# Normalisation, routing and row transfers of a sorted expert stage, moved into the attention before it

## The reference, cut to what matters

```python
x = x + _L1_xattn_ref(_layernorm(x), ctx, ctx, mask, ...)  # 16 heads of 64, keys 64 per batch
x = x + _L1_ffn_ref(_layernorm(x), ...)

def _L1_ffn_ref(x, gate_w, w1, w3, w2):     # 8 experts of width 512, two per token
    probs = softmax(x @ gate_w)
    expert_weights, expert_indices = top_k(probs, 2)
    expert_weights = expert_weights / expert_weights.sum(-1, keepdims=True)
    for i in range(8):
        wi = where(expert_indices == i, expert_weights, 0).sum(-1)
        out = out + (silu(x @ w1[i]) * (x @ w3[i])) @ w2[i] * wi[..., None]
```

## Time and profile before

| | us |
|---|---|
| median of 3 runs (lowest, highest) | 1563.43 (1560.48, 1563.63) |
| the profiled execution: its time | 1563.46 |
| its span, first to last instruction | 1561.6 |
| TensorE busy | 1265.0 (81%) |
| VectorE busy | 986.5 (63%) |
| ScalarE busy | 723.0 (46%) |
| GpSimd busy | 625.1 (40%) |

### The profile page before, as it was taken

One profiled execution on the slowest core, in us unless ns is written; L12 is line 12 of the kernel. 1 busy time (PEld: TensorE's weight loads), 2 busy tenths in 40 slices (PEclk: granted clock), 3 DMA queues, 4 the chain that ended last, 5 costly groups with the idle time before them and its releaser, 6 DMA issues. The chain is left out here.

```text
span 1561.6 us, 24205 instructions
## 1 busy us (share of the span) xinstructions
PE 1265.0 (81%) x7182; PEld 1030.1 (66%) x7182; DVE 986.5 (63%) x2041; ACT 723.0 (46%) x1276; POOL 625.1 (40%) x614
## 2 busy tenths in 40 slices
PE   5976499997996899712997596999945759999997
PEld 3873388887564699711886285788723548787875
DVE  6546688885324467560665655677668777777775
ACT  3444367664332555331554253555433325555553
POOL 3205443340000233154333332299824127676665
PEclk9997699997997999855999698799956569999999
DMA  7800011100000000221111620222212024343433
GB/s 202 205 1 0 21 36 41 40 25 0 0 1 0 21 1 0 81 100 52 40 45 32 174 42 21 69 81 87 83 42 84 1 73 129 114 129 116 126 116 102
DMA packets 77282, 98.89 MB, mean 63 GB/s; under 512 B 15226, under 2 KB 41213, under 8 KB 77194
## 3 DMA queue, kind: packets, MB, share of 16 engines
q1 hardware_dynamic: 73490, 92.69, 20.5%
q0 software_dynamic: 2272, 4.24, 0.8%
q10 hardware_dynamic: 1440, 0.98, 0.3%
HBM read 77.87 MB, written 14.16 MB: 59 GB/s over the span
## 5 line engine op out<-in xcount | busy, mean ns | idle before, releaser
L2675 POOL TENSOR_TENSOR e_h<-e_h,e_gate 128x512 f32<-128x512 f32 x128 | 187.9, 1484 | 143.8 <-DVE e_h L2727 87.9
L2732 DVE TENSOR_TENSOR e_h_low<-e_h,e_h_high 128x512 fp32r<-128x512 f32 x132 | 117.2, 888 | 74.4 <-ACT e_h_high L2662 74.2
L2662 ACT ACTIVATE e_h_high<-e_h 128x512 fp32r<-128x512 f32 x132 | 83.5, 633 | 95.8 <-POOL e_h L2675 88.1
L2727 DVE TENSOR_TENSOR e_h<-e_s,e_ps_b 128x512 f32<-128x512 f32 x132 | 89.3, 677 | 13.1 <-ACT e_s L2647 7.2
L1320 PE MATMUL u_ps_o<-u_vaug,u_pT 128*128 128x72 f32 x768 | 97.1, 270 | 0.0
L1320 PEld LDWEIGHTS u_ps_o<-u_vaug,u_pT 128*128 128x128 f32 x768 | 93.5, 192 | 0.0
L2647 ACT ACTIVATE e_s<-e_ps_a 128x512 f32<-128x512 f32 x132 | 77.7, 589 | 31.0 <-PE e_ps_a L1683 27.4
L1251 POOL TENSOR_TENSOR u_kbd<-u_keys,groupmask 96x512 fp32r<-96x512 f32 x60 | 62.9, 1067 | 62.4 <-DMA u_keys<-s_k 36.9
L1347 ACT ACTIVATE u_sm<-u_sm 128x512 f32<-128x512 f32 x96 | 60.6, 631 | 53.5 <-DVE u_sm L1379 52.8
L1377 DVE TENSOR_REDUCE u_mx<-u_ps_s 128x2 f32<-128x512 f32 (+1 forms) x96 | 66.2, 689 | 21.1 <-PE u_ps_s L1302 20.3
L2123 POOL DMA_INDIRECT sorted_y<-e_y,e_zb x39 | 37.8, 970 | 89.8 <-DVE e_y L2328 87.4
(11 more groups left out here) (474 smaller groups left out, 3894.4 us busy)
## 6 DMA issues: line engine op xcount, KB each, us to landing
e_gate<-gates_by_expert SPq DMA_DIRECT2D x256, 128.0 KB, 2.9
e_gate<-gates_by_expert SPq DMA_DIRECT2D x32, 256.0 KB, 3.2
a_q<-q_part SPq DMA_DIRECT2D x24, 256.0 KB, 6.4
w_raw<-in_L1w SPq DMA_DIRECT2D x24, 256.0 KB, 4.9
u_qs<-s_q SPq DMA_DIRECT2D x16, 192.0 KB, 2.6
u_keys<-s_k SPq DMA_DIRECT2D x8, 384.0 KB, 3.5
w_w<-in_L2w SPq DMA_DIRECT2D x24, 128.0 KB, 2.6
sorted<-blank SPq DMA_DIRECT2D x1, 2535.0 KB, 15.7
```

What stands on the lines that cost most here:

```text
L2662: nc.scalar.activation(h_parts[k % 3][0][:, :], h[k % 3][:, :], ACT.Copy).then_inc(high_ready, 1)
L2675: nc.gpsimd.tensor_tensor(h[c % 3][:, :], h[c % 3][:, :], gate[pair % SLOTS][:, :], ALU.mult)\
L2727: nc.vector.tensor_tensor(h[c % 3][:, :], s[c % 3][:, :], ps_b[c % 3][:, :], ALU.mult)\
L2732: nc.vector.tensor_tensor(h_parts[k % 3][1][:, :], h[k % 3][:, :], h_parts[k % 3][0][:, :], ALU.subtract).then_inc(low_ready, 1)
```

## The change

Layer norm, routing and transfers are taken apart into groups of four tiles and put into the steps of `attend_wide` by a new class `Router`, which each engine's program calls at (on TensorE: within) its step. Each expert has a fixed region of 2048 rows in `sorted`, so the place of a row needs only the counts of earlier groups; `table` gets a second row with each block's place in DRAM, which SP reads into a register for each block's load. The root becomes Ln and Exp on ScalarE with three operations on VectorE. To free a PSUM bank for the router, the transposes of the probabilities go through one bank in two halves. The blanks grow to 17280 rows. The wide attention's weights are loaded in the normalisation before it and no longer at the start of the program; the raw expert weights are loaded during the attention. Group 3 and the transfers from tile 8 on come after the attention. In the blocks, silu writes into `h`, there are four row buffers, TensorE spins on eight matmuls before the first rows, and a block waits only for the weights of the experts up to its own number.

```diff
+REGION = B * S
+SORTED_ROWS = SORT_E * REGION + (SORT_E - 1) * P
...
+class Router:
+    STEPS = 8
+    AFTER = 4
...
+    def dve(self, dve, t):
+        nc = self.nc
+        if 4 <= t < TILES + 4:
+            dve.drain()
+            nc.vector.bn_stats(self.stats[:, t - 4, :], self.x[:, t - 4, :])
+        if t % 4 == 3 and 7 <= t < TILES + 4:
+            self.variance(dve, (t - 7) // 4)
+        if t % 4 == 0 and 8 <= t < TILES + 8:
+            self.normal_rows(dve, (t - 8) // 4)
+        if t % 4 == 2 and 10 <= t < TILES + 8:
+            self.pick(dve, (t - 10) // 4)
+        if t % 4 == 3 and 11 <= t < TILES + 8:
+            self.places(dve, (t - 11) // 4)
+        if t == TILES + 7:
+            self.block_table(dve)
...
+    def normal_rows(self, dve, g):
+
+        nc, h = self.nc, self.tiles(g)
+        dve.wait_ge(self.root_ready, g + 1)
+        nc.vector.tensor_tensor(self.half[:, h], self.root[:, h], self.root[:, h], ALU.mult)
...
+        for t in range(h.start, h.stop):
+            last = nc.vector.tensor_scalar(self.rows[0][:, t, 0:D], self.x[:, t, :], self.mean[:, t:t + 1],
+                                           self.rstd[:, t:t + 1], ALU.subtract, ALU.mult)
+        last.then_inc(self.normed, 1)
+
+    def pick(self, dve, g):
+        nc, h = self.nc, self.tiles(g)
+        dve.wait_ge(self.logits_done, g + 1)
+        nc.vector.tensor_copy(self.flat(self.L, g), self.ps[:, 0:GROUP * SORT_E])
+        dve.drain()
+        for t in range(h.start, h.stop):
+            nc.vector.max(self.best[:, t, :], self.L[:, t, :])
+        dve.drain()
+        nc.vector.tensor_tensor(self.apart[:, h], self.best[:, h, 1], self.best[:, h, 0], ALU.subtract)
+        for t in range(h.start, h.stop):
+            nc.vector.max_index(self.who[:, t, :], self.best[:, t, :], self.L[:, t, :])
...
+    def places(self, dve, g):
+        nc, h, E = self.nc, self.tiles(g), SORT_E
+        n = GROUP * E
+        dve.wait_ge(self.ranked, g + 1)
+        nc.vector.tensor_tensor(self.place[:, h, :], self.ps[:, n:2 * n].rearrange("p (t e) -> p t e", e=E),
+                                self.base[:, :].unsqueeze(1).broadcast_to([P, GROUP, E]), ALU.add)
+        nc.vector.tensor_reduce(self.count[:, :], self.ps[:, 2 * n:3 * n].rearrange("p (t e) -> p e t", e=E), X, ALU.add)
+        dve.wait_ge(self.share_ready, g + 1)
...
+        nc.vector.tensor_tensor(self.base[:, :], self.base[:, :], self.count[:, :], ALU.add)
...
+        nc.vector.tensor_copy(self.index[:, h, :], self.slot[:, h, :]).then_inc(self.index_ready, 1)
...
+    def act(self, act, t):
+        nc = self.nc
+        if t % 4 == 0 and 8 <= t < TILES + 8:
+            g = (t - 8) // 4
+            h = self.tiles(g)
+            act.wait_ge(self.var_ready, g + 1)
+            nc.scalar.activation(self.root[:, h], self.var[:, h], ACT.Ln)
+            act.drain()
+            nc.scalar.activation(self.root[:, h], self.root[:, h], ACT.Exp, scale=-0.5).then_inc(self.root_ready, 1)
+        if t % 4 == 1 and 9 <= t < TILES + 8:
+            g = (t - 9) // 4
+            act.wait_ge(self.turned, g + 1)
+            nc.scalar.activation(self.zT[:, g * 512:(g + 1) * 512], self.ps[:, :], ACT.Copy).then_inc(self.z_out, 1)
+            h = self.tiles(g)
+            nc.scalar.activation(self.rows[1][:, h, 0:D], self.rows[0][:, h, 0:D], ACT.Copy).then_inc(self.copied, 1)
+        if t % 4 == 3 and 11 <= t < TILES + 8:
...
+            nc.scalar.activation(self.apart[:, h], self.apart[:, h], ACT.Exp).then_inc(self.share_ready, 1)
+
+    def pe(self, pe, t):
+        nc, E = self.nc, SORT_E
+        n = GROUP * E
+        if t % 4 == 1 and 9 <= t < TILES + 8:
+            g = (t - 9) // 4
+            pe.wait_ge(self.normed, g + 1)
+            if g > 0:
+                pe.wait_ge(self.index_ready, g)
...
+        if t % 4 == 2 and 10 <= t < TILES + 8:
+            g = (t - 10) // 4
+            pe.wait_ge(self.z_out, g + 1)
...
+        if t % 4 == 3 and 11 <= t < TILES + 8:
+            g = (t - 11) // 4
+            pe.wait_ge(self.picks_ready, g + 1)
...
+    def pool(self, pool, t):
+
+        if t < 12:
+            return
+        g, tile = (t - 12) // 4, t - 12
...
+        if t % 4 == 0:
+            pool.wait_ge(self.index_ready, g + 1)
+            pool.wait_ge(self.copied, g + 1)
+        for k in range(PICKS):
+            self.nc.gpsimd.indirect_dma_start(
...
                 if live(t, 3):
                     pe.wait_ge(p_ready, t - 2)
-                    wait(pe, pT_ready, t - 3)
...
+                for half in range(2):
+                    if live(t, 3):
+                        wait(pe, pT_ready, 2 * (t - 3) + half)
...
+                if router is not None:
+                    router.pe(pe, t)
                 if live(t, 4):
...
                 if live(t, 3):
-                    act.wait_ge(t_done, t - 2)
                     wait(act, o_done, t - 4)
-                    nc.scalar.activation(pT[1 - p][:, :, :].rearrange("p a b -> p (a b)"), ps_t[:, :], ACT.Copy)\
-                        .then_inc(pT_ready, 1)
+                    for half in range(2):
+                        act.wait_ge(t_done, 2 * (t - 3) + half + 1)
...
+                if router is not None:
+                    router.act(act, t)
...
+            sp.wait_ge(router.table_ready, 1)
             sp.wait_ge(scattered, 16 * PICKS * TILES)
...
+                for i in range(BATCH):
+                    j = q * BATCH + i
+                    row = sp.value_load(router.table[0:1, 1, j:j + 1], min_val=0, max_val=SORTED_ROWS - P)
+                    sp.dma_start(zb[q % NZ][:, i, :], sorted_dram[bass.ds(row, P), :]).then_inc(zb_loaded[q % NZ], 16)
...
+            for t in range(TILES + LAGS, TILES + Router.STEPS + Router.AFTER):
+                router.pool(pool, t)
...
+            for t in range(TILES + LAGS, TILES + Router.STEPS):
+                router.pe(pe, t)
+            pe.wait_ge(router.table_ready, 1)
+            pe.wait_ge(scattered, 16 * PICKS * TILES)
+            keep_busy(nc, ps_h[0], ones_b, 8)
             turn_rows(0)
...
+                if j < E:
+                    pe.wait_ge(weights.low_made, j + 1)
...
+            router.act(act, TILES + 4)
+            weights.make_high(act, 0)
+            router.act(act, TILES + 5)
+            weights.make_high(act, 1)
+            router.act(act, TILES + 7)
...
+            nc.vector.memset(scratch[:, :], 0.0).then_inc(scratch_ready, 1)
+            router.dve(dve, TILES + 4)
+            weights.make_low(dve, 0)
+            router.dve(dve, TILES + 6)
+            router.dve(dve, TILES + 7)
+            for e in range(1, E):
                 weights.make_low(dve, e)
...
-        normalise(nc, "n4_", x, idn, root_ln, zT, then=ACT.Exp)
...
+                normalise(nc, "n4_", x, idn, root_ln, zT, then=ACT.Exp,
+                          loads=load([(t, A["L1" + k]) for k, t in wide1.items()], wide_loaded))
...
+                arrive(nc, wide_loaded, 16 * len(wide1))
...
-            normalise(nc, "n5_", x, idn, root_ln, zT, gate_w=gate1, logits=logits[8], then=ACT.Exp,
-                      loads=weights.first_loads, rows=rows[0])
-            experts_sorted(nc, "e1_", x, logits[8], rank, sort, weights, idn, rows, drams[0],
-                           prefilled, signals[0])
```

More of the change, by code:

```diff
@@ L893, in step @@
                                             .broadcast_to([P, HEADS, KEYS]), ALU.mult).then_inc(p_ready, 1)
-            rotate(pool, step)
+                if router is not None:
+                    router.pool(pool, t)
+            rotate(step, LAGS)
         @block.tensor
@@ L947, in step @@
                     last.then_inc(vw_done, 1)
-            rotate(pe, step)
+            rotate(step, LAGS)
         @block.scalar
         def _(act):
+            if router is not None:
+                nc.scalar.preload_act_table_set("natural_log_exp_and_others")
             act.wait_ge(zeroed, 1)
@@ L2029, in experts_sorted @@
         m = Memory(nc, stack, tag)
-        sh = [P, TILES, E]
-        first, second, rest, key, place = (m.sb(n, sh) for n in ("first", "second", "rest", "key", "place"))
-        chosen = m.sb("chosen", sh, BF16)
-        mx1, mx2, top, share1, share2 = (m.sb(n, [P, TILES]) for n in ("mx1", "mx2", "top", "share1", "share2"))
-        slot = [m.sb(f"slot{k}", [P, TILES]) for k in range(PICKS)]
-        index = [m.sb(f"index{k}", [P, TILES], U32) for k in range(PICKS)]
-        count, over, ends, begins = (m.sb(n, [P, E]) for n in ("count", "over", "ends", "begins"))
-        summed_ends = m.sb("summed_ends", [P, E, E])
-        passed = m.sb("passed", [1, BLOCKS, E])
-        expert = m.sb("expert", [1, BLOCKS])
-        table = m.sb("table", [1, BLOCKS], I32)
         zb = [m.sb(f"zb{i}", [P, BATCH, ROW]) for i in range(NZ)]
@@ L2252, in _ @@
-            first_of_max(L[:, :, :], mx1, first)
-            nc.vector.scalar_tensor_tensor(out=rest[:, :, :], in0=first[:, :, :], scalar=-3.0e38, in1=L[:, :, :],
```

(15 more changed lines are left out.)

382 lines of the change are left out of this document (228 added, 154 removed).

## The result

The median of 4 runs is 1542.95 us (1538.38 to 1544.59) against 1563.31 before (1560.48 to 1563.63): ratio 0.9869, 95% interval 0.9845 to 0.9893, 20.4 us faster; 1536 was forecast. The profiled execution took 1544.59 us; its span is 1542.8, 18.8 less than that of before.

What follows compares the result with a forecast made beforehand. TensorE bounds the attention and expert blocks, but waits through the 84 us gap between. Span 1561.6 - 43.9 (gap) + 20.5 (attention) - 1.9 (clock) - 2.1 (buffers) + 0.4 (wait block) = 1534.6, so 1536 us; range 1511 to 1553, likeliest 1524 to 1548 (0.55).

Steps and rivals of the forecast that it cites:

- From E on: From the end of the attention's last addition to x (E) to the first expert matmul: 40.3 us instead of 84.2.
- What moves E: Router work and waits inside the attention delay the end of its last addition to x by 20.5 us.
- the steady steps: Attention's steady part: router work and waits cost 6.1 us a group, 12 for two groups.
- the tail: Attention's last four steps, where no projection hides anything: router work and waits add 8.5 us.
- TensorE's rank matmuls wait for the choice: Attention's last steps: rank matmuls ahead of the last output matmuls wait for expert choice, 2.4 and 0.6 us.
- The clock: Start of the expert blocks: eight spinning matmuls take it out of half clock, 1.9 us saved.
- Row buffers: Expert blocks: four row buffers instead of three remove waits of 2.1 us in all.
- the signs: Expected in the trace: last addition 15 to 25 us later, gap about 40, stalled transfers, TensorE waiting for ScalarE.
- Rival A: Router's VectorE work fits the attention's slack and last transfers meet no collision: 1514 us; under 1524 given 0.22.
- B: In the attention, VectorE's small operations wait behind GpSimd's multiplication, 11 us more: 1547; worst or longer stalls 0.13.
- C: Router waits queued in order lengthen thirteen attention steps from 7.7 to over 11.3 us, making the kernel slower; chance 0.06.
- D: Streaming does nothing: transfers remain one string behind the attention's last addition to x; no change given 0.04.

Runs made afterwards that it cites:

- experiment 1: Changed kernel with VectorE's weight subtractions held until all row transfers end and raw weights of experts 4 to 7 loaded behind the first row loads: 1544.52 us.
- experiment 2: Changed kernel with raw weights of experts 4 to 7 loaded behind the first row loads, experts 1 to 3 still subtracted beside the transfers: 1548.11 us.
- experiment 12: Changed kernel with router and key copies reordered, some transposes in a freed bank, and four small VectorE operations as breaks after each expert's subtractions: 1530.04 us.
- experiment 9: Changed kernel with router and key copies reordered, some transposes in a freed bank, weight subtractions moved behind the last transfer and into the blocks: 1528.15 us.
- experiment 5: Changed kernel with the whole router and all 32 transfers behind the attention, transposes still in two halves through one bank: 1561.59 us.
- experiment 3: Changed kernel with TensorE's router work in the attention's last four steps put behind the output matmuls: 1535.41 us.
- experiment 10: experiment 9 with TensorE spinning 40 matmuls from the block table on and 20 more behind the last transfer: 1525.47 us.
- experiment 6: Changed kernel with a spin of 24 matmuls instead of 8, started when the sixth expert's weights are split: 1543.30 us.
- experiment 11: Changed kernel with the 16 transfers of tiles 0 to 7 moved behind the attention, routing left in it: 1564.26 us.
- experiment 7: Changed kernel with 8, 8 and 12 spinning matmuls filling TensorE's waits in the attention's last three steps: 1539.30 us.

## Why the prediction was right, step by step

The forecast was 27 us faster, measured were 20.4, inside the range of the likeliest case (1524 to 1548) and with its mechanism. The span was forecast as 1534.6 and is 1542.8. The 8.2 between them are 1.4 from E on, 3.8 that E moves more, 1.5 in the blocks and 2.2 of slow clock near the start, less 0.7 in the rest. Terms in their order:

*From E on*, forecast 40.3, measured 41.7. The last indices came at E + 15.6 (15). The last eight transfers with their collision ended at E + 33.0 (32.7), and experiments 1, 2 and 12 show that it was VectorE's subtractions. From there to the first expert matmul it was 8.7 (7.6): the first load of rows starts 2.4 behind the last transfer and not 1.4, the rest took 6.3 (6.2). In this profile GpSimd waits 2.48 for the last indices, so the transfers of tiles 8 to 11 did fit in the room that the prediction saw for them. Where the last places come earlier (E + 13.8), as in experiments 1 and 9, GpSimd's own string is the limit: 16 transfers from E + 4.0 on at 1.27 end at E + 24.4, and these experiments end at 24.7 to 24.8.

*What moves E* is the mis-sized term: forecast 20.5, measured 24.3. It was made of wrong parts, and that it came so near is luck: the steady steps were put too high (12, measured 9.4), the tail too low (8.5, measured 14.9). In the steady steps the router cost 7.0 and the half bank 2.4: from tile 5 on the steps take 8.2 to 9.0 instead of 7.5 to 7.6. Of the 7.0, 4.1 are the waits for the evacuation in steps with key copies (1.74 and 2.39), and nearly all the rest is TensorE's own work for the router, 1.4 a group (0.44 for the transposes, 0.81 for the logits, 0.12 for the ranks) instead of 1.9; the forecast waits of 0.5 for the rows and 0.7 for the scores do not appear there. (The prediction's "four logit matmuls" are eight a group; its times, 1.8 and 0.9, are those of eight: 1.87 behind E and 0.81 in the attention.) What the attention pays without the router, 4.6 by experiment 5, the prediction knew only as part of a wait. In the tail (from the addition of tile 11 to E) 2.2 of the 14.9 are there without the router as well, and of the other 12.7 some 4.7 (16-matmul outputs at 3.62, 3.39 and 3.54 for 1.95) are the half clock that followed TensorE's waits. The step "TensorE's rank matmuls wait for the choice" was right in place and size (2.98 for 2.4 and 0.6), and experiment 3 shows that it was needless where it stood.

*The clock*, 1.9 forecast as saved, was 0: the spin of eight took 3.57 us, ran at half clock, and 1.49 of standing still came behind it. Experiment 10 shows that the term exists (2.3), experiment 6 that a spin which ends 4.00 too early does not bring it. *Row buffers*, 2.1 forecast: the waits of the earlier trace rows are gone and the blocks are 2.5 shorter; no run takes the fourth buffer away. *The wait block*, 0.4, took 0.38 (from ScalarE's last operation before the attention's stage to its first matmul 0.67 instead of 0.29). The blanks and the wide weights cost nothing that the trace shows.

Of the signs, E is 26.9 after its old place, 24.3 without the start and so inside 15 to 25; the gap, the one stalled transfer and the waits for ScalarE came as described.

Rival A (the attention absorbs the router) is refuted by the 19.7 of experiment 5. B (VectorE's small operations wait behind GpSimd's multiplication) had no experiment of its own, but the trace of the changed kernel answers it: none of the router's VectorE operations in the attention runs beside one of these multiplications, and the only idle times above 0.2 before one, three of 1.4, end with ScalarE's root. C would have needed 3.65 a step; in the steady steps it was 0.7 to 1.4. D is refuted by experiment 11, where the same transfers behind E lengthen the gap by 21.1.

Of the Trainium skill's lock (SBUF — State Buffer, "SBUF: two separate sides") the prediction said that by that rule a transfer would wait to the end of one operation. The runs agree that VectorE holds GpSimd's transfer off, and differ in the length: 5.25 to 7.50 us over six to eight operations without a break, and 1.76 to 1.78 with breaks. Which port or lock does it, no run here shows.

What stays open: VectorE's last places come 1.8 later in 4 of 12 profiles (the changed kernel and experiments 3, 6 and 7: E + 15.5 to 15.6, the others 13.8 to 14.0), with idle stretches of 1.35 and 0.39 us that no event in the trace releases; and why the clock falls near the start in some executions.

## What to carry to other kernels

Work that is streamed into a stage with little slack pays more with its waits than with its own busy time: put each of its instructions behind, not ahead of, what the bound engine has ready in the same step, above all in the last steps, where nothing else is queued. Where GpSimd issues transfers, keep long unbroken runs of VectorE subtractions like these away from them, or break the runs up. A spin that is to keep TensorE's clock has to reach up to the work that needs it: 4.00 us of standing still behind it lost the clock again in experiment 6, a wait of 1.25 behind the rows' transposes did not in experiment 10.

## What the runs showed of the hardware that was not expected

- One indirect transfer was held over a whole run of VectorE subtractions (7.03 us over eight, 5.25 over six) and ended 0.85 to 0.86 us after the run; four small operations with drains (0.85 us) were enough to let it out.
- TensorE's granted clock fell after it had waited 2.17 us in the attention's tail, from 1.00 to 0.77 and 0.71 in the next windows, and a 16-matmul output took 3.4 to 3.6 us instead of 1.95; with the waits filled by matmuls it stayed at 1.00. The Trainium skill, TensorE: Matmul & The Clock Gate, "HAM oscillation — how this bites in real kernels", says that standing still between bursts of matmuls brings the clock down; the runs agree: after 4.00 us of standing still the matmuls of experiment 6 ran at a pitch of 0.43, and with the waits filled those of experiment 10 ran at 0.23.
- The same instructions near the start (27 to 35 us) ran at 1.00 in some executions and at 0.53 to 0.65 in others, worth up to 2.2 us; why is not known. Two single profiles should be compared from a common instruction behind such a place.
